# Turning an expert block's gathered rows by one transposing DMA in place of eight TensorE transposes and a ScalarE copy

## The reference

```python
h = layernorm(x).reshape(T, D)                       # T = 2048, D = 512
scores = softmax(h @ gate_w.T); topk_w, topk_idx = top_k(scores, 6)   # of E = 16 experts
for e in range(16):                                  # MOE_D = 352
    out = (silu(h @ w_gate[e].T) * (h @ w_up[e].T)) @ w_down[e].T
    y = y + cw[:, e:e+1] * out                       # cw: the top-6 scores, 0 elsewhere
```

## Time and profile before

| | |
|---|---|
| three runs, us | 1927.49, 1928.22, 1937.55 (median 1928.22) |
| the profiled execution: its time, us | 1926.74 |
| the profiled execution: its span, us | 1925.0 |
| granted TensorE clock, mean over the span | 0.977 |

### The profile page before, as it was taken

How to read it: one execution, slowest core, us unless ns; L and a number is a source line. 1 busy time by engine, 2 the same in 40 slices (tenths; PEclk the granted TensorE clock), 3 DMA queues, 4 the chain that set the end, 5 groups by cost and what they waited for, 6 DMA issues and landing times.

```text
span 1925.0 us, 39526 instructions
## 1 busy us (share of the span) xinstructions
PE 1801.6 (94%) x12786; PEld 1073.8 (56%) x12789; DVE 1093.7 (57%) x2985; ACT 884.7 (46%) x1833; POOL 820.2 (43%) x731
## 2 busy tenths in 40 slices
PE   6989999999972999999999999995899999999998
PEld 3566666766631666666666666663554444444444
DVE  4578888888852323322322323223656877777776
ACT  4588888888841443444434434433732221122111
POOL 4234456656664344443433443442112444544442
PEclk9999999999985999999999999998999999999999
DMA  8255587777776666766665765545012355555653
GB/s 310 88 163 175 178 164 168 186 178 170 182 161 166 159 147 145 160 163 152 146 150 135 165 153 100 93 82 129 33 35 66 125 187 202 206 171 210 203 178 143
DMA packets 137921, 294.81 MB, mean 153 GB/s; under 512 B 39200, under 2 KB 64416, under 8 KB 133600
## 3 DMA queue, kind: packets, MB, share of 16 engines
q1 hardware_dynamic: 86752, 157.47, 29.5%
q0 software_dynamic: 46368, 126.29, 26.7%
q10 hardware_dynamic: 4608, 8.52, 1.5%
HBM read 426.00 MB, written 78.33 MB: 262 GB/s over the span
## 4 chain that ended last, share of the span: by engine, by line
PE 81%; DVE 6%; DMA 4%; issue 4%; ACT 3%; POOL 1%; SPq 0%; another core or an unknown queue 0%; ACTq 0%; POOLq 0%; DVEq 0%
PE bank L234 21%; PE bank L236 21%; PE bank L235 21%; PE bank L1061 3%; PE bank L1088 2%; PE bank L851 1%; DVE work_arena L1578 1%; DMA x_sum<-x,work_arena 1%; PE bank L927 1%; ACT xt_arena L1314 1%; PE bank L842 1%; POOL expert_tokens L2226 1%; DMA work_arena<-in_ctxT 1%; DMA work_arena<-in_pk_w 1%; DMA work_arena<-in_moe_w 1%
## 5 line engine op out<-in xcount | busy, mean ns | idle before, releaser
L234 PE MATMUL bank<-work_arena,xt_arena 128*128 x1221 | 404.7, 331 | 2.8 <-DVE xt_arena L2072 1.9
L235 PE MATMUL bank<-work_arena,xt_arena 128*128 x1221 | 404.6, 331 | 0.0
L236 PE MATMUL bank<-work_arena,xt_arena 128*128 x1221 | 404.5, 331 | 0.0
L2311 POOL DMA_INDIRECT x_sum<-x,work_arena x111 | 176.5, 1590 | 392.5 <-DMA x_sum<-x,work_arena 222.9
L2060 DVE TENSOR_TENSOR xt_arena<-xt_arena,bank 128x352 f32<-128x352 f32 x111 | 57.9, 522 | 405.9 <-PE bank L236 373.0
L234 PE MATMUL bank<-work_arena 128*128 128x512 f16 (+1 forms) x600 | 226.3, 378 | 15.1 <-DVE x L1883 6.8
L235 PE MATMUL bank<-work_arena 128*128 128x512 f16 (+1 forms) x600 | 226.4, 379 | 0.0
L236 PE MATMUL bank<-work_arena 128*128 128x512 f16 (+1 forms) x600 | 226.3, 378 | 0.0
L1468 ACT ACTIVATE xt_arena<-bank 128x1024 f16<-128x1024 f16 x111 | 113.6, 1023 | 224.4 <-PE bank L1061 212.0
L234 PE MATMUL bank<-xt_arena,work_arena 128*128 128x512 f16 x528 | 200.1, 379 | 1.7 <-DVE xt_arena L194 1.7
L235 PE MATMUL bank<-xt_arena,work_arena 128*128 128x512 f16 x528 | 200.1, 379 | 0.0
(11 more groups left out here) (278 smaller groups left out, 3823.0 us busy)
## 6 DMA issues: line engine op xcount, KB each, us to landing
work_arena<-expert_w SPq DMA_DIRECT2D x111, 1408.0 KB
work_arena<-expert_w SPq DMA_DIRECT2D x111, 768.0 KB
work_arena<-in_moe_w SPq DMA_DIRECT2D x64, 352.0 KB
expert_w<-work_arena SPq DMA_DIRECT2D x64, 352.0 KB
work_arena<-in_moe_w SPq DMA_DIRECT2D x64, 192.0 KB
expert_w<-xt_arena SPq DMA_DIRECT2D x64, 192.0 KB
work_arena<-in_mlp_w SPq DMA_DIRECT2D x8, 1536.0 KB
work_arena<-in_head_w SPq DMA_DIRECT2D x16, 512.0 KB, 5.6
```

The lines of the kernel that those rows point to most:

```text
L234: pe.matmul(o, a_hi, b_hi, start=start, stop=False)
L235: pe.matmul(o, a_hi, b_lo, start=False, stop=False)
L236: return pe.matmul(o, a_lo, b_hi, start=False, stop=stop)
L2311: pool.indirect_dma_start(out=xacc[:, :], out_offset=bass.IndirectOffsetOnAxis(ap=rid[:, i:i + 1], axis=0), in_=ysb[:, b % YB, :], in_offs ...
```

## The change

The eight transposes and the copy of a block go away. ScalarE issues one transposing DMA for each block instead: from `xb` (128 partitions by 1,024 float16) to `xT` (eight squares of 128x128, each turned). It is issued three blocks ahead, into four buffers instead of two. It waits for the block's gather, for up(b-4) (which frees its buffer), and for the transposing DMA of two blocks before. The gather into a buffer of `xb` now waits for the transposing DMA of the block six before. Bank 4 is free in this stage.

```diff
+XT_SLOTS, TURN_AHEAD = 4, 3
-        xT = er2.take(2, 8 * P, dt=F16)
+        er2.at = (er2.at + 7) // 8 * 8
+        xT = er2.take(XT_SLOTS, 8 * P, dt=F16)
+        xt_in = [sem(f"xt_in{s}") for s in range(2)]
...
-            def turn_rows(b):
-                pe.wait_ge(xb_in[b % XB], 16 * (b // XB + 1))
-                if b > 0:
-                    pe.wait_ge(xt_cp, b)
-                o = bank[4][:, :].bitcast(F16)
-                for i in range(8):
-                    m = pe.transpose(o[:, i * P:(i + 1) * P], xb[:, b % XB, i * P:(i + 1) * P], id16[:, :])
-                m.then_inc(xt_mm, 1)
...
             def expert_up(b, slot):
-                pe.wait_ge(xt_cp, b + 1)
+                pe.wait_ge(xt_in[b % 2], 16 * (b // 2 + 1))
...
-                        m = mm3(pe, o, xT[:, b % 2, d * P:(d + 1) * P], xT[:, b % 2, (DC + d) * P:(DC + d + 1) * P],
+                        m = mm3(pe, o, xT[:, b % XT_SLOTS, d * P:(d + 1) * P],
+                                xT[:, b % XT_SLOTS, (DC + d) * P:(DC + d + 1) * P],
...
-            turn_rows(0)
-            turn_rows(1)
             expert_up(0, slots[0])
             for b in range(NBLK - 3):
                 expert_up(b + 1, slots[b + 1])
                 slots[b + 2] = slot_of(b + 2)
-                turn_rows(b + 2)
                 turn_hidden(b)
...
-            def rows_copy(b):
-                act.wait_ge(xt_mm, b + 1)
+            def rows_turned(b):
+                act.wait_ge(xb_in[b % XB], 16 * (b // XB + 1))
+                if b >= XT_SLOTS:
+                    act.wait_ge(e_u, b - XT_SLOTS + 1)
                 if b >= 2:
-                    act.wait_ge(e_u, b - 1)
-                act.activation(xT[:, b % 2, :], bank[4][:, :].bitcast(F16), ACT.Copy).then_inc(xt_cp, 1)
+                    act.wait_ge(xt_in[b % 2], 16 * (b // 2))
+                act.dma_start(xT[:, b % XT_SLOTS, :].rearrange("p (c r) -> p c r", c=8), xb[:, b % XB, 0:8 * P],
+                              transpose=True).then_inc(xt_in[b % 2], 16)
...
-            rows_copy(0)
-            rows_copy(1)
+            for b in range(TURN_AHEAD):
+                rows_turned(b)
...
                 expert_silu(b + 1)
-                if b + 2 < NBLK:
-                    rows_copy(b + 2)
+                if b + TURN_AHEAD < NBLK:
+                    rows_turned(b + TURN_AHEAD)
                 hidden_high(b + 1)
...
                 if b >= XB:
-                    pool.wait_ge(xt_mm, b - XB + 1)
+                    pool.wait_ge(xt_in[b % 2], 16 * ((b - XB) // 2 + 1))
                     pool.wait_ge(e_cw, b - XB + 1)
```

More of the change, by code:

```diff
@@ L494, in build @@
         xb_in = [sem(f"xb_in{s}") for s in range(XB)]
-        xt_mm, xt_cp, e_g, e_u, e_sg, e_m, e_hh, e_hl, ht_mm, ht_cp, e_y, y_cp, e_cw = (
-            sem(f"e_{what}") for what in ("xt_mm", "xt_cp", "g", "u", "sg", "m", "hh", "hl", "ht_mm", "ht_cp", "y",
+        xt_in = [sem(f"xt_in{s}") for s in range(2)]
+        e_g, e_u, e_sg, e_m, e_hh, e_hl, ht_mm, ht_cp, e_y, y_cp, e_cw = (
+            sem(f"e_{what}") for what in ("g", "u", "sg", "m", "hh", "hl", "ht_mm", "ht_cp", "y",
                                           "y_cp", "cw"))
@@ L1119, in _ @@
             slots[NBLK - 1] = slot_of(NBLK - 1)
-            turn_rows(NBLK - 1)
             turn_hidden(NBLK - 3)
```

## The result

The change makes the kernel slower: 2013.52 us median of four runs (2008.52 to 2018.26) against 1929.74 (1927.49 to 1937.55), a ratio of 1.0426 with a 95% interval of 1.0400 to 1.0452. The forecast was 1941 us: right in sign, inside the wide range, and far too small, since the loss is some 82 us and not 13.

A forecast was written before the change was run, and what follows sets the result against it. TensorE bounds the loop, with the scatter chain close behind. Added traffic costs 36 us and freed TensorE time gives back 23, so 13 us more: 1941 us, range 1886 to 2140.

The forecast's parts named there:

- What bounds the kernel: In the loop: TensorE at 6.30 us a block, the scatter chain close behind at 6.22 loaded and 5.5 quiet.
- The freed 49 us, of which 23 would stay: Eight transposes off TensorE save 0.44 us for each of 111 blocks; the scatter chain leaves 23 us of that.
- backlog: Late scatters carried from the loaded stretch into the quiet one and made up there, a gain of 5 us.
- what the transposing DMA takes: Time of all sixteen DMA engines for a block: 0.89 us by bytes, taken; 6.4 us by packets as upper bound.
- The price of traffic: Each added megabyte lengthens the scatter chain 1.55 us: 0.41 us a block, 35 us loaded and 1 us quiet.
- The way to TensorE: In the loop, added DMA traffic lengthens the scatter chain, 0.41 us a block, and so holds up TensorE.
- the slow DMA: Rival: the transposing DMA takes over 2.1 us of the engines in the loaded stretch; 2270 us, chance 0.20.
- The new wait on ScalarE: ScalarE's queue now waits for the gather before the transposing DMA; 1.8 us of slack, no extra priced.
- The issue on ScalarE: Issuing the transposing DMA takes ScalarE at most 3.1 us a block, covered by the 4.2 us it has.
- The loop's start: First transposing DMA issued at 613.6 lands 2.5 to 4.9 us later; even within 2 us.
- the likeliest one: Case: the scatter chain takes over and is lengthened by traffic; 1922 to 1990 us, likeliest 1941, chance 0.44.
- The gain that comes through: Rival: transposing DMAs fall between scatters, adding 0.15 us or less to each; faster, 1900 us, chance 0.36.
- What the profile after would show: Signs: TensorE's quiet period 5.86 us, landing waits towards all scatters, mean above 3.35 us, DMA share up about 0.15.

The follow-up runs named there:

- no_turn: The changed kernel with no turning at all (gate and up from zeros, experts' part left out); 1911.73 us, ratio 0.9945 to the kernel before.
- no_turn_two_sums: The changed kernel without any turning, and with scatters alternating between two arrays; 1876.19 us, ratio 0.9722 to the kernel before.
- turn_beside: The kernel before plus a transposing DMA for each block into buffers that nobody reads; 1986.18 us, ratio 1.0300.
- plain_copy: The changed kernel with a plain DMA of the same bytes in place of the transposing one; 1947.87 us, ratio 1.0122 to the kernel before.
- copy_beside: The kernel before plus a plain DMA of 256 KB for each block into buffers that nobody reads; 1939.38 us, ratio 1.0078.
- half_beside: The kernel before plus an unread transposing DMA of four squares instead of eight (128 KB) for each block; 1959.72 us, ratio 1.0111.
- two_sums: The changed kernel with scatters of even and odd blocks into two arrays, odd blocks' part left out; 1965.69 us, ratio 1.0141 to the kernel before.
- start_on_pe: The changed kernel with blocks 0 to 2 turned by TensorE and copied as before, others by DMA; 1995.51 us, ratio 1.0318 to the kernel before.

## Why the prediction was right in sign and wrong in size

**What bounds the kernel** was read rightly: TensorE, with the scatter chain close behind it. no_turn and no_turn_two_sums show it, 11 us against 54.

**The freed 49 us, of which 23 would stay.** The 49 held. Of the 23 only 11 came. In the trace of no_turn the scatters of blocks 4 to 84 are 6.28 us apart, with TensorE freed, against 6.27 in the kernel before; from there on they are 5.67 against 6.17. So the quiet blocks gave 13 us, near the 11 of the sum and its 5 of backlog, and the loaded ones nothing: the chain already needed its whole period there. I had it at 6.22, with 0.08 to gain, because 15 intervals had to be guessed at 5.5.

**The step that failed: what the transposing DMA takes.** The prediction put it at 0.89 us of all sixteen engines, by bytes, "since shorter packets should take less than 0.10 us". They do, 27 ns, but 1,056 of them are 1.80 us (2.02 in turn_beside). By bytes is right for a plain DMA: 0.67 us. The two bounds, 0.89 and 6.4 us, held it, and I took the lower end itself instead of a value between them. How much this weighs can be worked out in the prediction's own terms: 0.41 us a block becomes 0.41*1.80/0.89 = 0.83, and the loaded interval 6.22 + 0.83 = 7.05 us; the trace has 7.06. That alone is 85*(7.05 - 6.30) = 64 us where the sum had 28, and 64 are what the trace shows from block 4 to block 84. The sum also had a slip of its own. It kept 5 us of backlog made up in the quiet stretch, where at 5.91 us against 5.86 there is no room left for it; without it the same prices give 18 us more and not 13.

**The price of traffic.** 1.55 us a megabyte, taken from the weights' stretch, gave 36 us for 29 MB. From no_turn to plain_copy it is 34 us, and plain_copy's scatters are 6.63 us apart from block 4 to 84 and 5.89 from there on, where the sum had 6.63 and 5.91. So the price held for a plain DMA in the changed kernel. It is no law: copy_beside, with the same bytes, lost 15 us, and by this price it should lose 0.33*85 = 28. copy_beside, half_beside and turn_beside lost 15, 21 and 58 us for 74, 104 and 224 us of all sixteen engines (111 blocks by 0.67, 0.94 and 2.02): a fifth to a quarter of the engines' time comes back as loss. This is measured for these three.

**The way to TensorE.** The prediction let the traffic reach TensorE by the scatter chain alone. The size fits, but two_sums does not bear the path out: without the chain 4.2 of the 4.8 points of the DMA's cost are still there. In the loop of the profile after TensorE's waits are for the turned rows themselves, 65.3 of 81 us, and that is the sign that the prediction gave for the slow DMA. A transposing DMA can be late because its gather was late (ScalarE's 438 us) or because it lands late itself (13.6 us after its issue at the start); both are seen, and the runs don't divide the cost between them.

**The new wait on ScalarE** was described with its slack of 1.8 us and priced at nothing. The view after shows 438 us of it, and easing it gave about a point. The issue on ScalarE, 1.25 us at its median, fitted into the 4.2 us as said. **The loop's start** was called even within 2 us. It cost 13.6 us from issue to first matmul in the profile after, by block 4 the loop was 25 us behind, and start_on_pe gained about a point. My range of 2.5 to 4.9 us for its landing came from DMAs that had the engines nearly to themselves.

**The clock** was not in the sum. The profile after grants 0.95 in the loaded stretch, where TensorE stops and starts. If all of what is missing is time at 1.2 GHz, that is a tenth of the stretch, and half of it lost work: some 30 us in 600. The busy time says the same: 11,901 matmuls took TensorE 1788.7 us, at a mean clock of 0.960, and 1747.6 us in no_turn_two_sums, at 0.982. That is 41 us which the sum did not have. Whether it adds to the loss, or only fills time that TensorE would have waited, no run separates.

**The rivals.** The slow DMA decided at 2.1 us of engine time in the loaded stretch; 1.80 to 2.02 is just short, at 0.86 to 0.94 busy engines. The true case lay between the likeliest one and this rival, which had a chance of 0.20. The gain that comes through needed under 0.15 us for each scatter; it was 0.88 by the waits (4.23 against 3.35). **What the profile after would show** came out in part: TensorE's period where it isn't held up is 5.85 us (its transposes of hidden halves at 1300.09 and 1305.94), the mean wait rose, and DMA share rose by 0.20 where I said 0.15. The waits for a landing did not rise towards all scatters: they are 51 of 71 (72%) after 62 of 81 (77%). In no_turn, where the chain is the bound, they do: 99 from 640 to 1300 us.

**What stays open:** why the single landings of the first transposing DMAs differ so (6.4 to 27.8 us in kernels whose starts are nearly alike), and by which way the DMA's cost reaches TensorE: what the 4.2 points are that it costs with two sums, late rows or full engines, and how much of the rest the chain carries. The edit of two sums was not tried beside turn_beside, which would say it for the traffic alone. No version tried here is faster than the kernel before and computes the reference.

## What to carry to other kernels

Before work is moved from a full engine to the DMA engines, price the transfer in time of the DMA engines, by its packets and what one of them takes (here 27 ns for a transposing DMA's, 0.67*16/144 = 74 ns for the plain one's), not by its bytes, and add it to the share that they have already. Then look for the chain that runs through DMA latencies: here accumulating scatters, each waiting for the last, left 11 of 54 us of freed TensorE time. To learn what such a chain carries of a new cost, take it away both with the new work and without it: the difference of the two, here 0.6 of 4.8 points, is its part, and not what the first edit gains. A wait put into an in-order queue, and the first use of a buffer while bulk loads start, are small terms that each cost a point.

## What was not expected of the hardware

- A transposing DMA of 128x1024 float16 from SBUF to SBUF is 1,056 packets of 27 ns, 1.80 to 2.02 us of all sixteen engines, against 144 packets and 0.67 us for a plain DMA of the same 256 KB.
- It holds ScalarE's queue for 1.25 us at its median, where a plain store took 0.39 us and the plain DMA of plain_copy 0.47 us. Half the size did not halve it: 1.21 us in half_beside.
- Beside the start of bulk loads of weights, the first one reached its user 6.4 to 27.8 us after its issue.

The row of its issues in the profile after (ns: min/median/max, first and last start):

```profile
L1461 ACTq DMA_TRANSPOSE xt_arena<-x x111: 1247/1251/7455, 615.9 to 1382.6; - x111
```
